# A Mamba block and a table-weight FFN on one core: own instruction orders for the two stages that decode the FFN's weights

## The reference, cut to what matters

```python
h  = layernorm(u)
z, x, B, C, dt = split(h @ W_in.T)
x, B, C = silu(causal_conv4(x, B, C) + conv_b)
dt = softplus(dt + dt_bias); dA = exp(dt * -exp(A_log))
S = S * dA_t + dt_t * B_t x_t ; y_t = S C_t + D x_t
x1 = u + layernorm((y * silu(z)) @ W_out.T)
h  = layernorm(x1)
out = x1 + layernorm((silu(h @ lut[gate_idx].T) * (h @ lut[up_idx].T)) @ lut[down_idx].T)
```

## Time and profile before

| what | value |
| --- | --- |
| median of 3 runs | 1434.93 us (1426.32 to 1438.0) |
| the profiled execution's own time | 1433.22 us |
| its span, first to last instruction | 1431.1 us |
| mean granted TensorE clock | 0.963 of full |
| PE busy | 1323.5 us (92%) |
| DVE busy | 964.0 us (67%) |
| ACT busy | 547.0 us (38%) |
| POOL busy | 521.2 us (36%) |

### The profile page before, as it was taken

The page is one execution under the profiler, slowest core; times in us unless marked ns, Lnnn a source line. Parts: engine busy times, 40 slices in busy tenths (PEclk is TensorE's granted clock), DMA queues, the critical chain, the costliest instruction groups (busy, mean ns, idle before and its releaser), DMA issues. The chain is left out here.

```text
span 1431.1 us, 18648 instructions
## 1 busy us (share of the span) xinstructions
PE 1323.5 (92%) x6656; PEld 636.8 (44%) x6656; DVE 964.0 (67%) x1895; ACT 547.0 (38%) x986; POOL 521.2 (36%) x723
## 2 busy tenths in 40 slices
PE   4759988988899999999999999999999999999998
PEld 2324434434444444454444444444444444444443
DVE  7977776887668766876687667765777466543432
ACT  5465565656443424342434224333333232122120
POOL 1413334432333453335433543453533444310102
PEclk9888889979999999999999999999999999999999
DMA  5143323521331233123311422123212211411201
GB/s 165 36 104 85 82 70 101 137 63 59 67 81 23 60 102 82 22 46 110 73 39 30 109 76 52 30 70 93 74 27 50 72 50 40 108 41 30 74 0 52
DMA packets 132812, 96.16 MB, mean 67 GB/s; under 512 B 102000, under 2 KB 102000, under 8 KB 132720
## 3 DMA queue, kind: packets, MB, share of 16 engines
q1 hardware_dynamic: 130832, 94.94, 25.4%
q10 hardware_dynamic: 1888, 0.03, 0.1%
HBM read 54.05 MB, written 16.78 MB: 49 GB/s over the span
## 5 line engine op out<-in xcount | busy, mean ns | idle before, releaser
L1328 PE MATMUL bank<-fxt,ffn_hi 128*128 128x512 f16 (+1 forms) x1408 | 422.8, 382 | 17.3 <-DVE gact L1657 15.4
L1328 PE MATMUL bank<-fxt,ffn_lo 128*128 128x512 f16 (+1 forms) x704 | 268.7, 382 | 0.0
L1328 PEld LDWEIGHTS bank<-fxt,ffn_hi 128*128 128x128 f16 (+1 forms) x1408 | 139.8, 101 | 190.9 <-DVE gact L1657 20.8
L1234 PE MATMUL bank<-mask,diag 128*128 128x416 f16 x640 | 140.0, 375 | 54.4 <-ACT ffn_lo L863 41.5
L638 POOL TENSOR_TENSOR state<-state,ex 64x512 f32<-64x512 f32 x32 | 35.5, 1108 | 329.2 <-PE bank L1291 328.2
L1342 PE MATMUL bank<-ffn_hi,h_hi 128*128 128x512 f16 (+1 forms) x352 | 133.5, 379 | 0.0
L1342 PE MATMUL bank<-ffn_hi,h_lo 128*128 128x512 f16 (+1 forms) x352 | 133.4, 379 | 0.0
L1342 PE MATMUL bank<-ffn_lo,h_hi 128*128 128x512 f16 (+1 forms) x352 | 133.3, 379 | 0.0
L603 POOL TENSOR_TENSOR decay<-causal_h,da 128x1024 f16<-128x1024 f16 x64 | 120.9, 1911 | 28.6 <-PE bank L1295 23.0
L1657 DVE SCALAR_TENSOR_TENSOR gact<-gact,bank 128x512 f32<-128x512 f32 (+1 forms) x88 | 60.2, 684 | 104.0 <-ACT gact L902 103.3
L1234 PEld LDWEIGHTS bank<-mask,diag 128*128 128x128 f16 x640 | 64.5, 105 | 131.9 <-ACT ffn_lo L863 48.2
(11 more groups left out here) (186 smaller groups left out, 2202.5 us busy)
## 6 DMA issues: line engine op xcount, KB each, us to landing
codes_sb<-codes SPq DMA_DIRECT2D x80, 208.0 KB, 3.4
ures<-u SPq DMA_DIRECT2D x32, 256.0 KB, 2.9
x_scratch<-x SPq DMA_DIRECT2D x32, 256.0 KB, 2.4
ut<-x_scratch SPq DMA_DIRECT2D x16, 512.0 KB, 4.4
xres<-x_scratch SPq DMA_DIRECT2D x32, 256.0 KB, 3.1
out<-dn SPq DMA_DIRECT2D x32, 256.0 KB, 2.0
ut<-u SPq DMA_DIRECT2D x15, 512.0 KB, 4.4
ffn_hi<-w_in_t SPq DMA_DIRECT2D x4, 580.0 KB, 8.7
```

The lines of the kernel that those rows point to most:

```text
L1234: last = nc.tensor.matmul(p.bank[:, 0:COLS], diag[:, q].rearrange("p n m -> p (n m)"), mask[:, n, q, j * COLS:(j + 1) * COLS], start=(q == ...
L1328: last = nc.tensor.matmul(bank, wt[:, c0:c0 + w], fxt[:, :, half, k, :], start=(k == 0 and n == 0), stop=(k == KC - 1 and n == 2))
```

## The change: what it does, and the diff

ACT and DVE get a function `decode_stage(t)` of their own for t = 0 and 1 (SP had one, which is reordered), and their `stage(t)` now serves only t of 2 and above. In the FFN stages the order on ACT and on SP stays as it was, and DVE's has one difference: `ln_stats("x", t - 1, 0)` and `time_steps(t + 1)` stand behind `times_up(g, 7)` and ahead of `gate_silu(g, 8)`.

In the decode stages, on ACT, `decoded(t, n)` stands ahead of `codes_to_half(k + n + 4)`, and `small`/`decays` right after the first or second of them. On DVE, `time_steps` moves from before `masks(k + 9)` to behind `masks(k + 10)`; `conv_silu` of blocks 2 and 3 stands behind a unit of masks; `z_gate(t + 1, 0)` moves from ahead of `y_gated(t, 3)` to behind `y_split(t, 3)`. The normalising of the next tile's slices begins one step earlier: the first pair of tile 1 in the prologue, that of tile 2 at the end of stage 0. On PE only `project_out(0, 0)` moves, behind `decode(0, 3)` and `decode(0, 4)`.

```diff
 SP, decode_stage(t)
+                    if t >= 1:
+                        transpose_pair("u", t + 1, 0)
                     load_codes(k + 6)
+                    transpose_y(t, 0)
                     load_codes(k + 7)
-                    transpose_y(t, 0)
...
+                    transpose_pair("u", t + 1, 1)
+                    if t + 1 < LAG:
+                        load_pair("u", t + 2, 0)
                     load_codes(k + 10)
...
+                    if t + 1 < LAG:
+                        load_pair("u", t + 2, 1)
                     if t >= 1:
                         transpose_pair("x", t - 1, 0)
                         transpose_pair("x", t - 1, 1)
-                    load_pair("u", t + 2, 0)
-                    load_codes(k + 24)
+                        load_pair("u", t + 2, 0)
                     load_codes(k + 25)
 ACT, normalise_slice
+                        if no == 2 and s == 0:
+                            act.wait_ge(xs_ready.sem, xs_ready.now(0, FB + 1))
 ACT
+                def decode_stage(t):
...
+                    decoded(t, 0)
+                    codes_to_half(k + 4)
+                    small(t, 1)
+                    decays(t, 1)
+                    decoded(t, 1)
+                    if t >= 1:
+                        normalise(t - 1, 3)
+                    codes_to_half(k + 5)
+                    if t >= 1:
+                        normalise_slice("u", t + 1, 1, 0)
+                        normalise_slice("u", t + 1, 1, 1)
+                    decoded(t, 2)
...
+                    decoded(t, 4)
+                    if t == 0:
+                        out_projected(t, 0)
+                        normalise_slice("u", t + 1, 1, 0)
+                        normalise_slice("u", t + 1, 1, 1)
+                    codes_to_half(k + 8)
+
+                    decoded(t, 5)
+                    dt_input(t + 1)
+                    conv_input(t + 1, 4)
+                    normalise(t, 0)
+                    dt_exponential(t + 1)
+                    codes_to_half(k + 9)
+                    small(t, 2)
+                    decays(t, 2)
+                    decoded(t, 6)
+                    conv_tanh(t + 1, 4)
+                    codes_to_half(k + 10)
+                    conv_input(t + 1, 0)
+                    decoded(t, 7)
+                    codes_to_half(k + 11)
+                    out_projected(t, 1)
+                    decoded(t, 8)
+                    conv_tanh(t + 1, 0)
...
+                    decoded(t, 18)
+                    codes_to_half(k + 22)
+                    if t + 1 < LAG:
+                        normalise_slice("u", t + 2, 0, 0)
+                        normalise_slice("u", t + 2, 0, 1)
...
                 codes_to_half(2)
+                normalise_slice("u", 1, 0, 0)
+                normalise_slice("u", 1, 0, 1)
                 codes_to_half(3)
-                for t in range(TILES):
+                for t in range(LAG):
+                    decode_stage(t)
+                for t in range(LAG, TILES):
                     stage(t)
 PE, stage(t)
-                    project_out(t, 0)
+                    if t > 0:
+                        project_out(t, 0)
                     if dec:
                         decode(t, 3)
                         decode(t, 4)
+                    if t == 0:
+                        project_out(t, 0)
 DVE
+                def decode_stage(t):
...
+                    decayed(t, 1)
+                    masks(k + 3)
+                    masks(k + 4)
                     if t == 0:
+                        ln_stats("u", t + 1, 1)
                         out_weights_low()
...
+                    conv_silu(t + 1, 4)
+                    masks(k + 9)
+                    conv(t + 1, 0)
                     if ffn_next:
                         ln_stats("x", t - 1, 0)
...
+                    conv_silu(t + 1, 0)
+                    masks(k + 10)
+                    time_steps(t + 1)
+                    masks(k + 11)
...
+                    conv_silu(t + 1, 1)
+                    conv(t + 1, 2)
+                    masks(k + 14)
+                    conv_silu(t + 1, 2)
+                    conv(t + 1, 3)
+                    masks(k + 15)
+                    conv_silu(t + 1, 3)
...
+                    y_gated(t, 3)
+                    y_split(t, 3, k + 17)
+                    z_gate(t + 1, 0)
+                    weigh(t + 1, 0)
+                    masks(k + 18)
...
 DVE, stage(t), t of 2 and above
+                    gate_silu(g, 7)
+                    low(g, 6)
+                    if nxt:
+                        conv_silu(t + 1, 0)
+                    times_up(g, 7)
+                    ln_stats("x", t - 1, 0)
+                    if nxt:
+                        time_steps(t + 1)
+                    gate_silu(g, 8)
```

More of the change, by code:

```diff
@@ L1706, in stage @@
                     y_gated(t, 0)
-                    if ffn:
-                        times_up(g, 0)
-                    y_split(t, 0, k + 2 if dec else None)
-                    if ffn and nxt:
+                    y_split(t, 0, k + 2)
+                    weigh(t, 1)
+                    if t == 0:
                         ln_split("u", t + 1, 0, 0)
                         ln_split("u", t + 1, 0, 1)
-                    if ffn:
-                        gate_silu(g, 1)
-                        low(g, 0)
-                        times_up(g, 1)
@@ new lines, in decode_stage @@
+                    masks(k + 5)
+                    if t == 0:
+                        ln_split("u", t + 1, 1, 0)
+                        ln_split("u", t + 1, 1, 1)
+                    masks(k + 6)
+                    y_sum(t, 1)
+                    out_stats(t, 0)
+                    y_gated(t, 1)
+                    y_split(t, 1, k + 7)
+                    dt_input(t + 1)
+                    conv(t + 1, 4)
+                    weigh(t, 2)
+                    masks(k + 8)
+                    decayed(t, 2)
@@ new lines, in decode_stage @@
+                    y_gated(t, 2)
+                    y_split(t, 2, k + 12)
+                    conv(t + 1, 1)
+                    weigh(t, 3)
+                    masks(k + 13)
+                    decayed(t, 3)
+                    conv_silu(t + 1, 1)
[5 more added lines that the diff above has]
+                    conv_silu(t + 1, 3)
+                    if ffn_next:
+                        ln_split("x", t - 1, 0, 0)
+                        ln_split("x", t - 1, 0, 1)
@@ new lines, in decode_stage @@
+                    masks(k + 19)
+                    z_gate(t + 1, 1)
+                    masks(k + 20)
+                    if t + 1 < LAG:
+                        ln_split("u", t + 2, 0, 0)
+                        ln_split("u", t + 2, 0, 1)
+                    if ffn_next:
+                        ln_split("x", t - 1, 1, 0)
+                        ln_split("x", t - 1, 1, 1)
+                        ln_stats("u", t + 2, 0)
+                    z_gate(t + 1, 2)
+                    z_gate(t + 1, 3)
@@ L1724, in stage @@
+                    masks(k + 21)
+                def stage(t):
+                    g = t - LAG
+                    nxt = t + 1 < TILES
+                    y_sum(t, 0)
+                    if t >= 1:
+                        out_stats(t - 1, 3)
+                    gate_silu(g, 0)
+                    y_gated(t, 0)
+                    times_up(g, 0)
+                    y_split(t, 0)
+                    if nxt:
                         ln_split("u", t + 1, 0, 0)
                         ln_split("u", t + 1, 0, 1)
-                        masks(k + 3)
@@ L1727, in stage @@
[L1727 to L1733 removed]
+                    gate_silu(g, 1)
+                    low(g, 0)
+                    times_up(g, 1)
+                    weigh(t, 1)
+                    if nxt:
+                        ln_stats("u", t + 1, 1)
+                    decayed(t, 1)
@@ L1749, in stage @@
+                    low(g, 2)
+                    times_up(g, 3)
+                    gate_silu(g, 4)
+                    low(g, 3)
+                    times_up(g, 4)
                     y_sum(t, 1)
                     out_stats(t, 0)
-                    if ffn:
-                        low(g, 4)
+                    low(g, 4)
                     y_gated(t, 1)
-                    y_split(t, 1, k + 7 if dec else None)
+                    y_split(t, 1)
                     if nxt:
```

380 lines of the change are left out of this document (147 added, 233 removed).

## The result

The changed kernel takes 1389.35 us (median of 4 runs, 1388.71 to 1390.11), the kernel before 1436.15 us beside it. The ratio is 0.969, with a 95% interval of 0.9651 to 0.9728. It is worked out from all runs and not from the two medians, whose quotient is 0.967. The forecast was 1384. The profiled execution took 1389.16 us with a span of 1387.0, so 44.1 us less than the profiled one before.

The account below looks back on a forecast made before the run. PE was taken to bound the FFN stages, DVE's work and waits the decode stages. Decode: 49.7 - 4 - 4 - 5 = 36.7 us; 1433.2 - 13.9 - 36.7 = 1382.6, with 1.7 us for the median 1384 us; range 1357 to 1414.

Parts of the forecast that it names:

- FFN stages: From stage 2 on: five PE waits of 2 us go (10.2 us) and three clock dips (3.7 us), together 13.9 us.
- A late mask holds up only a cast; so most of the 41.5 us go: Decode stages, ACT: with copies ahead of casts, PE's 41.5 us of waits for copies fall to under 12.
- z's tanh, 9.0 us: Decode stages, DVE: 9.0 of 12.8 us of waits go by moving z_gate behind y_split in slot 3.
- Layer norm slices, 3 of 6.8 us: Decode stages, DVE: 3 of 6.8 us of waits for slices go, as one pair of each tile is normalised ahead.
- y_sum, 15.7 us: Decode stages, DVE: waits at y_sum for the scan's products go, 11.5 + 4.2 = 15.7 us.
- Masks 7.8, gram 6.2 us: Decode stages, DVE: 7.8 us of masks waiting for PE to finish a unit and 6.2 us for the gram copy go.
- The convolution, 8 us: Decode stages, DVE: 8 of 5.0 + 4.6 us go; two of four conv_silu get a unit of masks before use.
- `conv_tanh` coming back, 4 us: Decode stages, ACT: conv_tanh(t + 1, 0) behind decoded(t, 8) costs 2 us in each stage, 4 us together.
- DVE and POOL, 5 us: Decode stages: some 12 us of POOL's work lose their cover and slow DVE; 8 us at most, 5 taken.
- The W_out wait, 4 us: Stage 0: second pair of tile 1 waits through project_out(0, 0) for W_out's low half; bounds 0 and 8, 4 us taken.
- Masks waits 20 to 30 us: Decode stages, forecast sign: PE's waits for masks grow from 12.9 to some 20 to 30 us.
- the load of `ut`: Decode stages, DVE: 7.7 us of waits for this load stay, as it has the same neighbours in stage 1.

Follow-up runs that it names:

- The probe: Kernel after, with eight spare POOL products added behind each of the eight weight preparations in stages 0 and 1: 1414.91 us, ratio 0.9896.
- copies and tanh: Kernel before, with ACT's copies ahead of the casts and each of the five conv_tanh behind the following unit's copies: 1431.08 us, ratio 0.9969.
- the pair of runs that both have SP's old order: Kernel after with early normalising and SP's order undone, ratio 0.9778; the same with casts also back ahead of the copies, ratio 0.9853.

## Why the prediction was right, and where its steps were not

The time (1389.35 for 1384) and the split (-32.2 for -36.7, -12.2 for -13.9) came out. The parts, each undone alone on the kernel after and read at stage 2, make up about as much: z's gate 13.8, early normalising with SP's order 12.0, copies' order 6.9, DVE's slots 0.9, together 33.6 us against the 31.7 by which stage 2 starts earlier. By the ratios the same four make 17.8, 12.6, 12.0 and 4.3, together 47 us, each with 5 to 6 us of doubt from after's own interval, so that they add up is read from single traces. The places of the tanhs on ACT, of `project_out(0, 0)` on PE and of `transpose_y` on SP were not undone by themselves. And they are not the parts that the forecast told of.

- **FFN stages.** Right: five waits of 2 us and all clock dips went, 11.2 us by the ratio and 16.2 in the trace when done alone. In after 4.0 us of that are lost, 3.8 of them in slot 0 of stage 2. There the statistics waited 4.42 us for `ut`, and PE 3.04 us behind them. I had not counted this.
- **"A late mask holds up only a cast; so most of the 41.5 us go".** This is the step that failed. I read the earlier trace rows as one blocked queue headed by the cast and gave it the whole stall. The queue had three heads: casts, layer norm slices and convolution tanhs. With the casts moved, PE still waited 29.9 us for copies behind the other heads. The 11.6 us that went came back as waits for masks (4.4 us more) and for the transposed y (7.2 us), whose transpose SP now issued late because its code loads wait for the casts. So the kernel was no faster. The 26.2 us directly behind slices were readable in the trace of before.
- **z's tanh, 9.0 us.** The mechanism was right and the size probably too small. DVE's waits fell from 12.8 to 0.4 us. The move brought 12.6 us by the ratio (9.4 at stage 2) on the kernel before, and undone on the kernel after it costs 13.8, with ACT's tanh in its new place. I had counted DVE's rest alone. In that run the masks behind it also ran slower beside POOL, and PE's busy time was 5.9 us longer in two slots.
- **Layer norm slices, 3 of 6.8 us.** Wrong: DVE's waits for them rose to 11.6 us. The part is worth up to 12.0 all the same, together with SP's order. DVE's wait was the wrong place to read it. ACT's queue isn't all of it either, as PE's waits for copies rose by only 1.8 us without it.
- **y_sum, 15.7 us.** Two rows of together 15.7 us fell to 2.6 and at most 0.5, as forecast.
- **Masks 7.8, gram 6.2 us.** The waits fell to 4.6 and 1.3 us, so 3.2 and 4.9 us went.
- **The convolution, 8 us, and `conv_tanh` coming back, 4 us.** Of 9.6 us of waits, 3.4 are left (2.57 and 0.84), both in front of `conv_silu(t + 1, 0)`, whose tanh stands behind `decoded(t, 8)`. So the 4 us were nearly right. DVE's order in slots 1 and 2 was worth 0 to 4 us in the run.
- **DVE and POOL, 5 us.** DVE's busy time in these stages rose by 6.4 us, and one mask from 410 to 434 ns. The probe shows that POOL's work lengthens DVE's; that all of the 6.4 us are this isn't shown. I also misread. For most of the 7.45 us POOL was at its full-precision products, and the cumulative ones began only at 67.81, 5.3 us after the masks.
- **The W_out wait, 4 us.** `project_out(0, 0)` waited 3.8 us, shown as "issue" in PE's waits. It ended 0.1 us behind the product that makes W_out's low half, which is read from the timeline and wasn't tried. The rest of DVE that I had forecast came: 3.33 and 0.52 us for the slices at 102.03 and 103.39.
- **"Masks waits 20 to 30 us".** Wrong place, nearly the right sum: masks 9.6 and the state update 10.9. DVE is late where the order puts its long pieces: with DVE's old slots the masks have 21.9 and the state 1.5.

That the total came so close is partly luck. On the rows of the sum DVE's waits fell from 58.9 to 24.4 us, so 34.5 net, where 49.7 - 4 - 4 = 41.7 were forecast; the load of `ut` fell by 4.9, which was to stay. Both sums are bounded by the same 76 us of rest, which is why the total was safer than the attribution. Nor is DVE's 248 us a fixed amount: the same work took 244.5 us with z's gate alone and 260.3 with copies and tanh. What stays open: how the gain of 7 to 12 us from the copies' order, which is nothing on the kernel before, divides among its partners. The tanh's place is one (4.4 us together by the ratio on the kernel before), and SP's `transpose_y` may be another. It can't be all of it, since the copies' order was worth 9.5 us in the pair of runs that both have SP's old order. The largest stall left behind a slice, 3.68 us at 237.47, wasn't tried.

## What to carry to other kernels

When an engine's queue is blocked, list everything between the blocked head and the work that is needed, for every long stall, before pricing a move. Taking one head away can give the time to the next one. Look at the other engines' queues too: a step moved back on one engine is a later release for another, as with the casts and SP's loads.

Price a wait by what it sets off (the masks behind it, the starved PE, its clock), not by its own length. What a part brings alone on the old kernel and what undoing it alone costs on the new one can differ, as with the copies' order (0 and 7 to 12 us); try both, and check that the undoing takes back nothing else.

An instruction that waits for a late chain (statistics, a tanh) belongs behind the work that another engine is short of. For z's gate this gained clearly. For `ln_stats` behind `gate_silu` the waits went, while the ratio's interval leaves the gain open.

## What the runs showed of the hardware that I had not expected

POOL's product of 128 x 256 half-precision numbers took 738 ns, while one of 128 x 1024 took 1958 ns in the same run, so four small ones cost half as much again as a large one. The 47 us of small ones made a DVE that was busy for nearly 90% of the time 0.67 us longer per us. The masks went from 434 to 505 ns in the mean.

PE's busy time for the same matmuls of two slots was 67.75 us where PE starved once for 4.60 and once for 4.38 us, and 61.85 where its longest stall was 2.53 us. The waits aren't the whole difference between two such kernels.
